# A state-space block's X, turned by DMA instead of TensorE, and its step size moved into exponents

## The reference

```python
x = causal_conv(input @ Wx.T) ; x = silu(x) ; z = input @ Wz.T      # 4 taps, 512 channels
b, c = x @ Wb.T, x @ Wc.T                                            # 8 heads x 64 states
dt = softplus(x @ Wdt.T + b_dt) ; a = -exp(log_a)                    # one a head
state = exp(dt_t * a) * state + (dt_t * b_t) x_t                     # for each token t
y_t = c_t . state ; y = y + d_param * x
out = (group_norm(y) * silu(z)) @ Wout.T
x = x + layernorm(out) ; x = x + layernorm(ffn(layernorm(x)))
```

## Time and profile before

| | |
|---|---|
| median of 3 executions | 1281.62 us (1279.63 to 1281.98) |
| the profiled execution | 1279.33 us, span 1277.6 us |
| granted TensorE clock | 0.99 of full speed |
| PE busy | 1221.6 us (96%) |
| PE weight loads busy | 761.1 us (60%) |
| DVE busy | 995.7 us (78%) |
| ACT busy | 879.5 us (69%) |
| POOL busy | 470.8 us (37%) |
| DMA, share of 16 engines | 15.1% |

### The profile page before, as it was taken

The page is one execution under the profiler, slowest core; times in us unless marked ns, Lnnn a source line. Parts: engine busy times, 40 slices in busy tenths (PEclk is TensorE's granted clock), DMA queues, the critical chain, the costliest instruction groups (busy, mean ns, idle before and its releaser), DMA issues. The chain is left out here.

```text
span 1277.6 us, 27524 instructions
## 1 busy us (share of the span) xinstructions
PE 1221.6 (96%) x10260; PEld 761.1 (60%) x10260; DVE 995.7 (78%) x2381; ACT 879.5 (69%) x1554; POOL 470.8 (37%) x561
## 2 busy tenths in 40 slices
PE   6998999999999999999999999999999999999986
PEld 4564656566475655647566565756656575664753
DVE  6575778969777887877779787887878779697676
ACT  6564686677876687766877668667787668776355
POOL 2040434324361434416343253523336152441333
PEclk9999999999999999999999999999999999999988
DMA  8020201102021110201111020111202111020001
GB/s 236 1 68 1 35 18 34 35 18 67 17 42 44 34 34 17 67 18 35 38 26 55 17 68 17 35 34 26 59 17 55 30 18 34 18 67 17 2 1 50
DMA packets 91829, 48.08 MB, mean 38 GB/s; under 512 B 63121, under 2 KB 89893, under 8 KB 91697
## 3 DMA queue, kind: packets, MB, share of 16 engines
q1 hardware_dynamic: 91696, 46.33, 15.1%
HBM read 22.72 MB, written 8.39 MB: 24 GB/s over the span
## 5 line engine op out<-in xcount | busy, mean ns | idle before, releaser
L934 POOL TENSOR_TENSOR Cd<-Cd,CT 128x512 f32<-128x512 f32 x64 | 94.1, 1471 | 371.1 <-ACT Cd L1177 370.7
L1718 PE MATMUL bank<-sh,WbT 128*128 128x512 f16 x768 | 175.5, 385 | 4.5 <-DVE sh L1305 3.8
L1718 PE MATMUL bank<-sh,WcT 128*128 128x512 f16 x768 | 171.3, 379 | 0.0
L1205 ACT ACTIVATE hf<-bank,vectors,alpha 128x512 f32<-128x512 f32 x128 | 99.2, 777 | 56.6 <-PE bank L1912 32.0
L1300 DVE SCALAR_TENSOR_TENSOR xs<-xi,vectors,xs 128x512 f32<-128x512 f32 x168 | 125.1, 749 | 9.6 <-ACT xs L1082 5.9
L1718 PEld LDWEIGHTS bank<-sh,WbT 128*128 128x128 f16 x768 | 73.4, 99 | 92.6 <-DVE sh L1305 7.9
L1718 PEld LDWEIGHTS bank<-sh,WcT 128*128 128x128 f16 x768 | 75.2, 98 | 86.6
L1912 PE MATMUL bank<-uh,sign1T 128*128 128x512 f16 x512 | 123.7, 385 | 2.8 <-ACT uh L1200 1.6
L1929 PE MATMUL bank<-sign2T,hh 128*128 128x256 f16 x1024 | 119.5, 275 | 4.2 <-DVE hh L1540 4.1
L1929 PEld LDWEIGHTS bank<-sign2T,hh 128*128 128x128 f16 x1024 | 98.1, 99 | 26.7 <-ACT hf L1205 6.5
L865 POOL TENSOR_TENSOR rstd_mid<-var_eps_mid,power 128x4 f32<-128x4 f32 x16 | 16.2, 1011 | 227.3 <-DVE var_eps_mid L1255 227.3
(11 more groups left out here) (232 smaller groups left out, 2590.2 us busy)
## 6 DMA issues: line engine op xcount, KB each, us to landing
xt<-L_attn_input_tensor_dram SPq DMA_DIRECT2D x17, 512.0 KB, 4.5
u<-L_attn_input_tensor_dram SPq DMA_DIRECT2D x15, 512.0 KB, 3.9
out_dram<-u SPq DMA_DIRECT2D x15, 512.0 KB, 3.0
yT<-in_L_ffn_w_dram SPq DMA_DIRECT2D x2, 512.0 KB, 8.4
u<-in_L_ffn_w_dram SPq DMA_DIRECT2D x2, 512.0 KB, 8.8
BT<-in_L_attn_Wx_dram SPq DMA_DIRECT2D x1, 512.0 KB, 5.2
BT<-in_L_attn_Wz_dram SPq DMA_DIRECT2D x1, 512.0 KB, 4.6
zs<-in_L_attn_Wb_dram SPq DMA_DIRECT2D x1, 512.0 KB, 6.3
```

Of the source, the lines that this page charges most:

```text
L934: pool.tensor_tensor(Cd[n % 2][:, :, :], Cd[n % 2][:, :, :], CT[:, :, q * P:(q + 1) * P], ALU.mult)\
L1205: nc.scalar.activation(hf[f % 2][:, :], bank(t, ("H", j, f))[:, :], ACT.Gelu, bias=b1_col[:, f:f + 1], scale=alpha1[:, f:f + 1]).then_inc( ...
L1718: mm = nc.tensor.matmul(bank(t, key)[:, :], w[i][:, k, cols(m)], v[h][:, k, :], start=(a == 0), stop=(a == len(terms) - 1))
```

## The change

Each chunk's X with tokens as rows is no longer made by TensorE out of the 32-bit `xs`. `sh` is laid out chunk by chunk, SP transposes the high and the low half of a chunk by DMA (`turn_tokens`, step "X") into two tiles inside `xi` that chunks 0 and 2, and 1 and 3, share, and VectorE sums the halves into `xdt`, which now holds 256 x instead of dt x. The step size enters as ln(dt / 256): once in the product that makes cum (`log_wide`), so that the mask holds it, and once in the sums, so that the decay to the chunk's end holds it. For that VectorE puts a floor under dt, ScalarE takes the logarithm, and VectorE writes it out (`step_wide`). The Gelu table is loaded behind that logarithm, in j = 0 blocks behind two steps of the group norm instead of before them. The bank that "X" had is a gap in the ring; the other uses keep their banks.

```diff
             steps += weights(("rows", 0))
-        steps += own(("log", j))
-        steps += tail(("mid_norm", j)) + own(("B", j, 1), ("decay", j)) + tail(("gelu_table",))
-        steps += tail(*[("fold", 1, m) for m in range(2 if j == 0 else 0)], ("ff_stat", j))
+        steps += own(("X", j, 0), ("X", j, 1), ("log", j))
+        steps += tail(("mid_norm", j)) + own(("B", j, 1), ("decay", j)) + tail(*[("fold", 1, m) for m in range(2 if j == 0 else 0)])
+        steps += own(("ln_dt", j)) + tail(("gelu_table",), ("ff_stat", j)) + own(("ln_wide", j))
         if j == 0:
...
             steps += weights(("w1", 2), ("w1", 3), ("alpha1", 0))
-        steps += own(("score", j, 1), ("carry", j, 0)) + norm + (own(("head_stat", 0, 0)) if j else [])
+        steps += own(("X", j, 2), ("score", j, 1), ("X", j, 3), ("carry", j, 0)) + norm + (own(("head_stat", 0, 0)) if j else [])
         steps += out[1] + own(("back", j, 0)) + xT
...
         xi = sb("xi", [P, KI, XI_ROW])
+        x_turned = [xi[:, KI - 1 if r else 0, 0:BLK].bitcast(F16).rearrange("p (i c f) -> p i c f", i=2, c=KI) for r in range(2)]
         turn = [xi[:, 1 + i, 0:BLK].bitcast(F16).rearrange("p (k q d) -> p k q d", k=KD, q=NQ) for i in range(2)]
...
         xs = sb("xs", [P, KI, BLK])
-        sh = [sb(f"sh{i}", [P, KI, BLK], F16) for i in range(2)]
+        sh_rows = [sb(f"sh{i}", [P, NQ, KI, P], F16) for i in range(2)]
+        sh = [v[:, :, :, :].rearrange("p q c t -> p c q t") for v in sh_rows]
         zs = sb("zs", [P, KI, T])
...
             return sb(name, [P, NQ, HEADS], dt)
-        v_dt, abs_v, exp_v, one_e, e_back, e_rest, log_u = (small(n) for n in (
-            "v_dt", "abs_v", "exp_v", "one_e", "e_back", "e_rest", "log_u"))
+        v_dt, exp_v, one_e, e_back, log_u = (small(n) for n in ("v_dt", "exp_v", "one_e", "e_back", "log_u"))
+        abs_v, e_rest = exp_v, e_back
         dt_raw = small("dt_raw")
...
         da = sb("da", [P, NQ * HEADS])
+        dt_floor, log_dt = dt_raw, log_u
+        log_wide = sb("log_wide", [P, HP, PARTS, NQ * KI])
         da_wide = sb("da_wide", [P, HP, PARTS, NQ * KI])
...
             if kind == "seg":
-                return [*[("seg", *at, g) for g in range(HP)], ("X", *at), ("Bt", *at)]
+                return [*[("seg", *at, g) for g in range(HP)], None, ("Bt", *at)]
             if kind == "E":
...
+            def turn_tokens(t, j, q):
+                n = ch(j, q)
+                r = q % 2
+                s, sj, sq = two_before(t, n)
+                if q == 0:
+                    sp.wait_ge(*conv_out.count(t, (j + 1) * KI * (TAPS - 1)))
+                    sp.wait_ge(*sh_hi.count(t, (j + 1) * KI))
+                    sp.wait_ge(*sh_lo.count(t, (j + 1) * KI))
+                sp.wait_ge(*xdt_out.count(s, ch(sj, sq) + 1))
+                for i in range(2):
+                    sp.dma_start_transpose(x_turned[r][:, i, :, :], sh_rows[i][:, q, :, :].rearrange("p c t -> p (c t)")).then_inc(x_rows[r].sem, 16)
...
                 s, sj = before_block(t, j)
-                act.wait_ge(*full(s, ("X", sj, NQ - 1)))
                 act.wait_ge(*sh_lo.count(s, (sj + 1) * KI))
...
                     act.wait_ge(*xi_out.count(s, (sj + 1) * KI))
+                    act.wait_ge(*xdt_out.count(s, (sj + 1) * NQ))
                     if not (opening(t) and j == 0):
...
                     act.wait_ge(*full(s, ("C", sj, KI - 1)))
-                nc.scalar.activation(sh[0][:, c, :], xs[:, c, :], ACT.Copy, scale=SX).then_inc(sh_hi.sem, 1)
+                    for landed in x_rows:
+                        act.wait_ge(*landed.count(s, (sj + 1) * NQ // 2))
+                nc.scalar.activation(sh[0][:, c], by_chunk(xs[:, c, :]), ACT.Copy, scale=SX).then_inc(sh_hi.sem, 1)
...
             def step_log(t, j):
+                p, pj = before_block(t, j)
+                act.wait_ge(*full(p, ("sums", pj)))
+                act.wait_ge(*ln_wide.count(p, (pj + 1) * HP))
                 act.wait_ge(*dt_step.count(t, j * DT + 3))
...
+            def step_size_log(t, j):
+                act.wait_ge(*ln_in.count(t, j + 1))
+                nc.scalar.activation(log_dt[:, :, :], dt_floor[:, :, :], ACT.Ln, scale=1.0 / SX).then_inc(ln_out.sem, 1)
...
                 dve.wait_ge(*sh_hi.count(t, j * KI + c + 1))
-                nc.vector.scalar_tensor_tensor(out=sh[1][:, c, :], in0=xs[:, c, :], scalar=SX, in1=sh[0][:, c, :],
+                if c == 0:
+                    s, sj = before_block(t, j)
+                    for landed in x_rows:
+                        dve.wait_ge(*landed.count(s, (sj + 1) * NQ // 2))
+                nc.vector.scalar_tensor_tensor(out=sh[1][:, c], in0=by_chunk(xs[:, c, :]), scalar=SX, in1=sh[0][:, c],
                                                op0=ALU.mult, op1=ALU.subtract).then_inc(sh_lo.sem, 1)
...
                 s = j * DT
+                p, pj = before_block(t, j)
                 dve.wait_ge(*dt_act.count(t, j * 2 + 2))
+                dve.wait_ge(*ln_out.count(p, pj + 1))
                 nc.vector.scalar_tensor_tensor(out=dt_raw[:, :, :], in0=v_dt[:, :, :], scalar=0.0, in1=log_u[:, :, :],
...
                 dve.wait_ge(*da_seen.count(t, j + 1))
-                p, pj = before_block(t, j)
                 dve.wait_ge(*full(p, ("sums", pj)))
+                nc.vector.tensor_scalar(dt_floor[:, :, :], dt_t[:, :, :], DT_FLOOR, None, ALU.max).then_inc(ln_in.sem, 1)
                 raw = da_raw[:, :, :].rearrange("p q h -> p (q h)")
...
+            def step_wide(t, j):
+                p, pj = before_block(t, j)
+                dve.wait_ge(*full(p, ("cums", pj)))
+                dve.wait_ge(*ln_out.count(t, j + 1))
+                raw = log_dt[:, :, :].rearrange("p q h -> p (q h)")
+                for g in range(HP):
+                    v = of_side(raw, g)[:, None].to_broadcast([P, PARTS // 2, NQ * KI // 2, 2])
+                    nc.vector.tensor_scalar(log_wide[:, g, PARTS // 2:PARTS, :].rearrange("p m (n f) -> p m n f", f=2), v, -1.0, None,
+                                            ALU.mult).then_inc(ln_wide.sem, 1)
...
-                for need in latest(full(t, ("X", j, q)), full(s, ("Y", sj, sq, HP - 1))):
-                    dve.wait_ge(*need)
+                dve.wait_ge(*full(s, ("Y", sj, sq, HP - 1)))
                 dve.wait_ge(*xdw_out.count(s, ch(sj, sq) + 1))
-                nc.vector.tensor_tensor(xdt[r][:, :, :], heads(bank(t, ("X", j, q))[:, :]), per_head(dt_t[:, q, :]),
-                                        ALU.mult).then_inc(xdt_out.sem, 1)
+                dve.wait_ge(*x_rows[q % 2].count(t, n // 2 + 1))
+                hi, lo = [x_turned[q % 2][:, i, :, :].rearrange("p c f -> p (c f)") for i in range(2)]
+                nc.vector.tensor_tensor(xdt[r][:, :, :], heads(hi), heads(lo), ALU.add).then_inc(xdt_out.sem, 1)
...
                         pe.wait_ge(*ready(k))
-                    mm = nc.tensor.matmul(bank(t, key)[:, :], w[i][:, k, cols(m)], v[h][:, k, :], start=(a == 0),
+                    mm = nc.tensor.matmul(by_chunk(bank(t, key)[:, :]), w[i][:, k, cols(m)], v[h][:, k], start=(a == 0),
                                           stop=(a == len(terms) - 1))
...
                 nc.tensor.matmul(bank(t, key)[:, 0:P], da_wide[:, :, :, :].rearrange("p g a n -> p (g a n)"), upto[:, :],
-                                 start=True, stop=True).then_inc(full_sem(t, key), 1)
+                                 start=True, stop=False)
+                pe.wait_ge(*ln_wide.count(t, (j + 1) * HP))
+                nc.tensor.matmul(bank(t, key)[:, 0:P], log_wide[:, :, :, :].rearrange("p g a n -> p (g a n)"), ident[:, :],
+                                 start=False, stop=True).then_inc(full_sem(t, key), 1)
...
                 pe.wait_ge(*empty(t, key))
-                nc.tensor.matmul(bank(t, key)[:, 0:NQ * HEADS], after[:, :], da[:, :], start=True, stop=True)
+                nc.tensor.matmul(bank(t, key)[:, 0:NQ * HEADS], after[:, :], da[:, :], start=True, stop=False)
+                pe.wait_ge(*ln_out.count(t, j + 1))
+                nc.tensor.matmul(bank(t, key)[:, 0:NQ * HEADS], ident[:, :], log_dt[:, :, :].rearrange("p q h -> p (q h)"),
+                                 start=False, stop=True)
                 for g in range(HP):
...
                     mm.then_inc(full_sem(t, key), 1)
-                for name, src in (("X", xs), ("Bt", BT)):
-                    key = (name, j, q)
-                    for need in latest(empty(t, key), B_out.count(t, (j + 1) * KI), C_out.count(t, (j + 1) * KI)):
-                        pe.wait_ge(*need)
-                    for c in range(KI):
-                        mm = nc.tensor.transpose(bank(t, key)[:, cols(c)], src[:, c, cols(q)], ident[:, :])
-                    mm.then_inc(full_sem(t, key), 1)
+                key = ("Bt", j, q)
+                for need in latest(empty(t, key), B_out.count(t, (j + 1) * KI), C_out.count(t, (j + 1) * KI)):
+                    pe.wait_ge(*need)
```

(18 more changed lines are left out.)

16 lines of the change are left out of this document (8 added, 8 removed).

## The result

The changed kernel takes 1293.93 us (median of 4, 1293.6 to 1294.49) against 1281.33 us for the kernel before, measured beside it: ratio 1.0101, 95% interval 1.0083 to 1.0118. So it is 1% slower; the forecast was 1294.6, slower. The profiled execution took 1293.8 us around a span of 1292.1, which is 14.5 us more than before's 1277.6.

What follows compares the result with a forecast made beforehand. TensorE, busy 1221.6 of 1277.6 us, was taken as the bound, with some work covering waits on other engines. +13 (thirteen blocks) + 0.6 (first batch) - 0.5 (last block) = +13 on 1281.6 gave 1294.6 us, range 1272 to 1303.

Steps and rivals of the forecast that it cites:

- The deciding step: Chunk stage: xdt, now adding two SBUF tensors, and GpSimd's products hold each other up; main case, chance 0.52.
- the rival without a collision: Chunk 2: 16-bit reads don't hold GpSimd up, so xdt starts right behind L1290; -6, 1276 us; chance 0.20.
- the two bounds of the prediction: The new xdt's own length on VectorE: between 0.42 us (L1390) and 0.69 us (the old xdt), nearer the latter.
- steps 2 to 4: From chunk 2's hand-over on, Bt of chunk 3 starts 0.77 us later in j=0 blocks, 0.53 in j=1 blocks.
- step 2: Chunk 2: L1290 (L1327 after the change) ends at 517.90, waiting Cd goes first until 519.12, xdt ends +1.13 us later.
- Step 1: Chunk 1: all runs 0.43 us early until xdt pushes Cd 0.6 us later: +0.17 against before, ScalarE's exponentials too.
- Two products a block: TensorE, from B and C up to H: 0.46 us lost in j=0 blocks, 0.24 in j=1 blocks, mean 0.35.
- DMA transposes, the strided moving operand, the small instructions: SP's queue, B and C on TensorE, VectorE's floor and small products, ScalarE's logarithm: hidden by cover, costing nothing.
- What X's removal is worth: TensorE loses X's transposes: 0.43 us won in chunk 0, nothing more in chunk 1, at most 0.2 in chunk 3.
- Steady batches: Each batch costs 0.77 + 0.24 + 0.53 + 0.46 = 2.0 us; thirteen blocks of this form give +13.
- First batch: No tail stands behind mt there, so the delay is mostly absorbed: +0.3 us a block, +0.6 together.
- Last block: No next input, so no L1290; TensorE keeps about 1.0 us against 0.46 of products: -0.5 us.

Runs made afterwards that it cites:

- one_psum: The changed kernel with xdt as the product of a PSUM bank and the broadcast step size instead of the sum of two SBUF halves: 1278.32 us.
- no_dma_transposes: The changed kernel without its 128 DMA transposes of X, xdt summing the halves unturned as they lie in sh: 1295.4 us.
- x_back_on_pe: The changed kernel with TensorE's transposes of X put back at their old place and bank, read by nobody: 1303.44 us.
- xdt_before_low: The changed kernel with xdt of chunk 2 moved on VectorE ahead of the subtraction making the next input's low half: 1288.94 us.
- mt_first: The changed kernel with the two mt products of chunk 2 moved on VectorE ahead of xdt: 1306.77 us.
- low_after_mt: The changed kernel with the subtraction making the next input's low half (L1327) moved behind xdt and mt of chunk 2 on VectorE: 1301.07 us.
- gpsimd_xdt: The changed kernel with GpSimd instead of VectorE summing the two turned halves into xdt: 1300.49 us.

## Why the prediction was right, and where its sizes were off

- **The deciding step, xdt with two SBUF operands, is shown.** Its hand-over behind L1327 was forecast with a duration of about 1.9 us and an end 1.13 us later than before; it lasts 1.76 us and ends at 526.79, 26.42 us into the block, where before it was 518.62 - 493.04 = 25.58: 0.84 later. one_psum takes it away, and the time lands at 1278.32, where the rival without a collision had 1276. Alone, the new xdt takes 0.675 us, at the upper of the two bounds of the prediction; no xdt came near the lower one, 0.42. The Trainium skill ("SBUF — State Buffer", section "SBUF: two separate sides") describes an exclusive lock on a shared pair of ports, asked for by VectorE instructions with two SBUF inputs against a GpSimd one that reads SBUF; the runs agree, xdt at 0.68 us with an operand in PSUM and up to 1.77 without. When both waited, the hand-over went as in the earlier trace rows: Cd, waiting when L1327 ended, went ahead of xdt (1.76 us).
- **Size of steps 2 to 4.** Bt of chunk 3 was to be +0.77 us in j = 0 and is +0.47 (29.97 against 29.50 us into the block); its scores are +0.53. In j = 1 blocks Bt of chunk 3 is at +0.27 for a forecast of +0.53, its scores at +0.33. The j = 1 block that was to be about 1 us longer than 566.60 to 643.95 runs from 574.62 to 652.75, 0.78 longer. In step 2 the replay had L1327 end 0.1 us too late, Cd take 0.1 too long after it, and xdt take 0.1 too long after Cd; the 0.3 together went through undamped.
- **Step 1.** Bt and the scores of chunk 1 start 0.43 us early, as forecast. xdt pushes Cd of chunk 1, which ends 17.01 us into the block against 16.99 before: +0.02, where +0.17 was forecast. The scores of chunk 2 are at +0.02 too. So step 1 costs next to nothing.
- **Two products a block:** 0.70 us a pair forecast, 0.76 measured by leaving them out.
- **DMA transposes, the strided moving operand, the small instructions: nothing.** For the transposes this is shown (no_dma_transposes), for the rest only read: B's and C's products have a mean of 383 and 379 ns, 385 and 379 before. Though half the size, an X transpose holds the queue as long as the others, 1.27 us (median) for the 1.23 of the earlier trace rows, and lands 2.6 us later. The cover was 5 us.
- **What X's removal is worth.** 1.52 us more a pair, less 0.76 for the products and 2.03 for the collision, leaves -1.27 for it, if the three simply add: 0.63 us a block, where the prediction had 0.70. From the other side, with the collision in place, x_back_on_pe has 1.09 a pair. The 1.96 us of transposes a block mostly filled waits, as the earlier trace rows said.
- **That the sum came within 0.7 us is in part luck: two errors cancel.** Steady batches: 2.0 us forecast, 1.52 measured, 3 us too much over 6.5 pairs. First batch: +0.6 forecast; from the first step size's product to that of batch 1 it takes 139.06 us for 134.68, +4.4, after a start 0.6 us earlier, so 3.8 net. Last block: -0.5 forecast, +0.5 measured (from the last batch's first such product to the end 202.25 us for 200.73, of which 1.0 is the delay of a j = 0 block as in the batches before). Most of what is missing in the first batch and the last block is of one kind, which the prediction did not have: TensorE's clock.

TensorE's granted clock (the column behind the busy times; full is 1.00, half is the lower level, 1.2 GHz), in windows of the kernel after and, under it, of the kernel before:

```profile
core 0: us, PE busy (x) PEld busy (x) DVE busy (x) ACT busy (x) POOL busy (x), PEclk, DMA share, GB/s
76.00:80.00 4.00, 3.83 (x50) 3.31 (x50) 3.33 (x4) 0.98 (x3) 2.55 (x2) 0.57 0.55 83
...
1196.00:1200.00 4.00, 3.70 (x25) 2.66 (x26) 1.63 (x3) 2.15 (x5) 2.35 (x3) 0.58 0.39 70
```

```profile
76.00:80.00 4.00, 3.91 (x69) 3.16 (x70) 2.90 (x7) 1.04 (x3) 3.04 (x3) 1.00 0.78 76
...
1182.00:1186.00 4.00, 3.26 (x32) 2.42 (x34) 2.03 (x4) 3.21 (x8) 3.32 (x3) 1.00 0.00 0
```

The timeline of the kernel after shows what the engine did ahead of it and what it cost:

```profile
76.17 1.90 PE L1886 MATMUL bank<-CT,BT 64*128 64x128 f32 x16 [1.71 <-ACT mt L1204]
...
141.44 2.08 PE L1886 MATMUL bank<-CT,BT 64*128 64x128 f32 x16 [1.49 <-ACT mt L1204]
...
1196.30 2.08 PE L1886 MATMUL bank<-CT,BT 64*128 64x128 f32 x16 [3.46 <-ACT mt L1204]
```

From the scores to the output of chunk 2 it takes 3.82 us and 3.71 us in the first batch where the kernel before took 2.31 and 2.30: 2.9 of the 4.4 us. In the last block the scores of chunk 1 follow those of chunk 0 after 4.00 us; before it was 3.09, with 0.59 for X: 1.5 us. From 322 to 1074 us the granted clock is 1.00 in both kernels, so the steady pairs hold none of this.

## What to carry to other kernels

Before a VectorE operand is moved out of PSUM, look for a GpSimd product beside it: with both operands in SBUF it did the same work here in 0.675 to 1.77 us, as it had to wait for GpSimd's product or not, and everything in its queue moved with it. Follow both chains that leave such a place, the engine's own queue and the data's way over the other engine; four of the experiments here (xdt_before_low, mt_first, low_after_mt, gpsimd_xdt) missed because one of the two, or the scores that limit mt, was left out. And work that is taken off the busiest engine is worth only what does not fill a wait, here about 1.3 of 3.9 us a pair.
